# A quad's products reordered (rounded values first, low half last, two waits) and the weight preparation moved some steps later

## The reference

```
y      = layernorm(x), split in 16 heads of 8 columns
scores = y_h y_h^T / sqrt(8)             per batch and head, 1024 x 1024
o_h    = softmax(scores) @ y             y with all 128 columns
attn   = concat_h(o_h) @ weight          weight is (16*128, 128)
x      = x + layernorm(attn)
y      = layernorm(x); xr, xk = mixes of y and of y one row earlier
ffn    = sigmoid(xr W_r^T) * (relu(xk W_k^T)^2 W_v^T)
out    = x + layernorm(ffn)
```

## Time and profile before

| | us |
|---|---|
| median of 3 runs | 944.18 (943.57 to 948.45) |
| the profiled execution | 950.29 |
| span of its instructions | 948.5 |
| PE busy in the span | 914.9 (96%) |
| DVE busy | 850.3 (90%) |
| ACT busy | 753.4 (79%) |
| POOL busy | 320.2 (34%) |

### The profile page before, as it was taken

How to read it: one execution, slowest core, us unless ns; L and a number is a source line. 1 busy time by engine, 2 the same in 40 slices (tenths; PEclk the granted TensorE clock), 3 DMA queues, 4 the chain that set the end, 5 groups by cost and what they waited for, 6 DMA issues and landing times.

```text
span 948.5 us, 17874 instructions
## 1 busy us (share of the span) xinstructions
PE 914.9 (96%) x6065; PEld 441.9 (47%) x6065; DVE 850.3 (90%) x1117; ACT 753.4 (79%) x1048; POOL 320.2 (34%) x485
## 2 busy tenths in 40 slices
PE   3999999999999999999999999999999999999995
PEld 2444444444544444444444444544544444444453
DVE  7889898899898899989988979989889899898887
ACT  6787878788778778888778887889787978788855
POOL 2111432441143613515115282443313451153501
PEclk9999999999999999999999999999999999999999
DMA  5899999989889888999988978899988989889840
GB/s 162 195 225 188 205 197 200 226 190 204 177 173 201 163 181 174 208 193 207 185 178 179 203 157 179 176 222 202 206 173 180 188 182 188 172 179 201 174 81 24
DMA packets 98698, 173.12 MB, mean 183 GB/s; under 512 B 21040, under 2 KB 61360, under 8 KB 98608
## 3 DMA queue, kind: packets, MB, share of 16 engines
q0 software_dynamic: 36720, 133.71, 72.3%
q1 hardware_dynamic: 61888, 38.28, 14.7%
HBM read 27.72 MB, written 10.49 MB: 40 GB/s over the span
## 4 chain that ended last, share of the span: by engine, by line
PE 80%; issue 5%; POOL 4%; DVE 4%; DMA 4%; ACT 4%; DVEq 0%; POOLq 0%; ACTq 0%
PE ps_o L610 22%; PE ps_o L612 20%; PE ps_o L611 20%; PE ps_s L591 7%; DMA e_hi<-e_f 3%; PE ps_r L625 3%; PE ps_r L627 3%; PE ps_r L626 3%; ACT e_f L776 2%; DVE e_lo L1129 1%; POOL zT L452 1%; POOL e_hi L433 1%; PE ps_x L652 1%; PE ps_x L648 1%; POOL fnw L411 1%
## 5 line engine op out<-in xcount | busy, mean ns | idle before, releaser
L1129 DVE TENSOR_TENSOR e_lo<-e_f,e_hi 128x2048 f16<-128x2048 f32 x256 | 586.1, 2290 | 62.2 <-DMA e_hi<-e_f 62.1
L776 ACT ACTIVATE e_f<-ps_s 128x2048 f32<-128x2048 f32 x256 | 481.6, 1881 | 133.8 <-PE ps_s L591 124.4
L610 PE MATMUL ps_o<-e_hi,y_hi 128*128 128x512 f16 x1024 | 390.7, 382 | 6.3 <-DVE o_neg L1135 4.7
L612 PE MATMUL ps_o<-e_hi,y_lo 128*128 128x512 f16 x1024 | 388.1, 379 | 0.0
L611 PE MATMUL ps_o<-e_lo,y_hi 128*128 128x512 f16 x1024 | 388.1, 379 | 0.0
L433 POOL DMA_DIRECT2D e_hi<-e_f x255 | 140.9, 553 | 571.1 <-ACT e_f L776 469.8
L610 PEld LDWEIGHTS ps_o<-e_hi,y_hi 128*128 128x128 f16 x1024 | 99.7, 97 | 155.0 <-issue 56.1
L788 ACT ACTIVATE part<-ps_r,rden 128x128 f32<-128x128 f32 x508 | 144.8, 373 | 33.3 <-DVE rden L1141 32.6
L612 PEld LDWEIGHTS ps_o<-e_hi,y_lo 128*128 128x128 f16 x1024 | 100.2, 98 | 120.9
L611 PEld LDWEIGHTS ps_o<-e_lo,y_hi 128*128 128x128 f16 x1024 | 100.4, 98 | 91.5 <-issue 0.7
L591 PE MATMUL ps_s<-op_t,op_s 32*128 32x512 f16 x1024 | 102.5, 388 | 2.9 <-ACT e_f L776 2.4
(11 more groups left out here) (235 smaller groups left out, 507.4 us busy)
## 6 DMA issues: line engine op xcount, KB each, us to landing
e_hi<-e_f POOLq DMA_DIRECT2D x255, 512.0 KB, 5.1
op_t<-scr_t SPq DMA_DIRECT2D x496, 32.0 KB, 3.7
op_s<-scr_s SPq DMA_DIRECT2D x496, 16.0 KB, 3.3
scr_s<-yT SPq DMA_DIRECT2D x12, 256.0 KB, 2.9
scr_t<-yT SPq DMA_DIRECT2D x12, 256.0 KB, 5.4
out_dram<-res SPq DMA_DIRECT2D x7, 256.0 KB, 4.6
xs<-in_L_attn_x_dram SPq DMA_DIRECT2D x3, 512.0 KB, 6.2
scr_s<-eighth SPq DMA_DIRECT2D x4, 256.0 KB, 4.4
```

The lines of the kernel that those rows point to most:

```text
L610: nc.tensor.matmul(dst, y_hi[:, b % 2, s, :], e_hi[:, ring, g, :], start=(q == 0 and g == 0), stop=False)
L612: mm = nc.tensor.matmul(dst, y_lo[:, b % 2, s, :], e_hi[:, ring, g, :], start=False, stop=(q == 1 and g == 3))
L776: nc.scalar.activation(e_f[:, k % EF_RING], ps_s[:], ACT.Exp, scale=1.0 / ROOT).then_inc(weighed, 1)
L1129: dve.tensor_tensor(flat(e_lo[:, ring]), flat(e_f[:, k % EF_RING]), flat(e_hi[:, ring]), ALU.subtract).then_inc(split, 1)
```

## The change

Four things change, and the line numbers of the changed kernel are 4 to 11 higher than before.

1. **Products.** Of a quad's twelve matmuls the eight that read only `e_hi` come first, then the four that read `e_lo`. At the start PE now waits for the cast's DMA (`cast_in`, or `rounded` for quad 0), and a second wait, for `split`, stands ahead of the last four. `cast_count` is the count that DVE waited for before.
2. **Opening on PE.** `products(0)` moves from pass 4 to pass 3, ahead of the second `first_operands`; the four `weights_less` move behind it, the last one to pass 6; they use other banks, and `weight_sum` moves from pass 6 to pass 7.
3. **Weight preparation.** On DVE the four `weight_base` move to k = 3 to 6, `weight_scale` from k = 6 to 8, `weights_low` from 8 to 10. On ACT `keep_weight_sum` moves from 6 to 8, `weights_high` from 7 to 9, `weights_neg` from 8 to 10.
4. **`step_at`.** Step 0 now comes at lead+2, step 1 at lead+3, step 2 at lead+4: `project` at k = 10, 11, 12 (before 9, 10, 12), `invert` and `scale` at 11, 12, 13 (before 10, 11, 13).

```diff
         def weights_ps(i):
-            return (ps_o[:, 1, :], ps_o[:, 1, :], ps_r[:], ps_x[:])[i]
+            return (ps_o[:, 1, :], ps_r[:], ps_x[:], ps_r[:])[i]
 
         def step_at(k, lead):
 
-            if k == lead + 1:
-                return 0
-            return (k - lead) // 2 if k > lead and (k - lead) % 2 == 0 else None
+            if k in (lead + 2, lead + 3):
+                return k - lead - 2
+            return (k - lead) // 2 if k > lead + 3 and (k - lead) % 2 == 0 else None
...
+        def cast_count(k):
+
+            return 16 * (k // EH_RING + (k % EH_RING > 0))
...
                 if i == 1:
-                    pe.wait_ge(w_based, 1)
+                    pe.wait_ge(first_s_in, 2)
                 if i == 2:
-                    pe.wait_ge(first_s_in, 2)
+                    pe.wait_ge(first_t_in, 3)
                 if i == 3:
-                    pe.wait_ge(first_t_in, 3)
+                    pe.wait_ge(w_based, 2)
...
             def products(k):
                 j, q = k // 2, k % 2
                 b, ring = batch_of(j), k % EH_RING
-                pe.wait_ge(split, k + 1)
+                if k == 0:
+                    pe.wait_ge(rounded, 1)
+                else:
+                    pe.wait_ge(cast_in[ring], cast_count(k))
...
                 for g in range(4):
                     s = 2 * g + q
                     nc.tensor.matmul(dst, y_hi[:, b % 2, s, :], e_hi[:, ring, g, :], start=(q == 0 and g == 0), stop=False)
-                    nc.tensor.matmul(dst, y_hi[:, b % 2, s, :], e_lo[:, ring, g, :], start=False, stop=False)
-                    mm = nc.tensor.matmul(dst, y_lo[:, b % 2, s, :], e_hi[:, ring, g, :], start=False,
+                    nc.tensor.matmul(dst, y_lo[:, b % 2, s, :], e_hi[:, ring, g, :], start=False, stop=False)
+                pe.wait_ge(split, k + 1)
+                for g in range(4):
+                    mm = nc.tensor.matmul(dst, y_hi[:, b % 2, 2 * g + q, :], e_lo[:, ring, g, :], start=False,
                                           stop=(q == 1 and g == 3))
                 mm.then_inc(product, 1)
...
                 if k == LAG - 1:
+                    products(0)
+                    first_operands(1)
                     weights_less(0)
-                    first_operands(1)
+                if k == LAG:
                     weights_less(1)
-                if k == LAG:
                     weights_less(2)
-                    weights_less(3)
-                if 0 <= k - LAG < QUADS:
+                if 1 <= k - LAG < QUADS:
                     products(k - LAG)
                 if k == LAG + 2:
+                    weights_less(3)
+                if k == LAG + 3:
                     weight_sum()
...
-                if k == 6:
+                if k == 8:
                     keep_weight_sum()
-                if k == 7:
+                if k == 9:
                     weights_high()
-                if k == 8:
+                if k == 10:
                     weights_neg()
...
-                    weight_base(0)
-                    weight_base(1)
-                if k in (3, 4):
-                    weight_base(k - 1)
-                if k == 6:
+                if 3 <= k < 7:
+                    weight_base(k - 3)
+                if k == 8:
                     weight_scale()
-                if k == 8:
+                if k == 10:
                     weights_low()
```

More of the change, by code:

```diff
@@ L528, in weight_sum @@
                 pe.wait_ge(w_based, 3)
-                nc.tensor.matmul(ps_r[:, 0:1], ones[:], w_sum[:, 0:1], start=True, stop=True).then_inc(w_total, 1)
+                nc.tensor.matmul(ps_x[:, 0:1], ones[:], w_sum[:, 0:1], start=True, stop=True).then_inc(w_total, 1)
             def first_operands(n):
@@ L603, in products @@
                     if j == 1:
-                        pe.wait_ge(w_based, 2)
+                        pe.wait_ge(w_based, 1)
                     if j % (2 * H) == 0:
@@ L851, in keep_weight_sum @@
                 act.wait_ge(w_total, 1)
-                nc.scalar.activation(w_sum[:, 1:2], ps_r[:, 0:1], ACT.Copy).then_inc(w_summed, 1)
+                nc.scalar.activation(w_sum[:, 1:2], ps_x[:, 0:1], ACT.Copy).then_inc(w_summed, 1)
             def normalize_half():
@@ L1126, in split_quad @@
                 else:
-                    dve.wait_ge(cast_in[ring], 16 * (k // EH_RING + (ring > 0)))
+                    dve.wait_ge(cast_in[ring], cast_count(k))
                 ge(dve, product, k - EH_RING + 1)
```

## The result

| | us |
|---|---|
| changed kernel, median of 4 runs | 957.83 (955.8 to 958.6) |
| kernel before, median of 4 runs | 944.84 (943.57 to 948.45) |
| ratio, 95% interval | 1.0118 (1.0091 to 1.0145) |
| changed kernel, profiled execution | 957.83, span 956.0 |

A forecast was written before the change was run, and what follows sets the result against it. The prediction took PE, busy for 96% of the span, as the bound. Its terms, 0 (steady part) + 0.7 (opening) + 6.1 (first projection) = +6.8 us, on 944.2 gave 951.0 us, range 946.0 to 955.0.

The forecast's parts named there:

- The bound: Whole kernel: PE, busy for 96% of the span, sets the time; a 512-column matmul starts every 0.2155 us.
- Order and waits: Steady part: the new product order and its two waits cost 0, with 1.4 us of gain as the end.
- the wait for `e_lo` comes back at `o_neg`: Steady part: PE saves 1.38 us at `e_lo` but gives it back at `o_neg`, behind that `e_lo` in DVE's queue.
- The opening: Start to score group 8: early products run at the low clock; +0.7 us taken, between -1.0 and +1.5.
- The first projection: Score groups 8 to 13: `project(0)` waits 4.4 us for `w_lo`, later projections wait too; +6.1 us, from +4.6 to +8.6.
- the cast of quad 8: Ahead of `w_lo` in DVE's queue: the cast's DMA lands 5.8 us after issue, the median; fastest 4.3, slowest 8.3.
- The third projection: `project(2)` at k = 12 waits 2.5 us for `scale(1)`, which stands behind `f_turned` and `take_o(3)` on ACT.
- Against it: the gap is a little shorter than the one seen.: Ahead of `project(0)`: the 4.4 us gap is under the 4.6 us after which the clock fell at the end.
- Rival (a): Gap before `project(0)`: the clock falls to 1.2 GHz and PE loses 2.7 us more, 953.7 us; chance 0.20.
- The median of the runs lies 6.1 us below that execution; the difference carries over.: Whole kernel: +6.8 us gives 957.1 on the 950.3 us profiled execution, so 951.0 on the 944.2 us median.

The follow-up runs named there:

- order_only: The kernel before with only the new order of a quad's products and its two waits; ratio 1.0012 (0.9993 to 1.0031).
- twelve_waits: order_only with twelve more satisfied waits in each quad but the first, one ahead of each product; 946.75 us, ratio 0.9997 against the kernel before.
- opening_only: The changed kernel with the old order and old single wait of the products; ratio 1.0070 against the kernel before.
- low_k9: The changed kernel with `weights_low` one pass earlier on DVE (k = 9 instead of 10); 951.50 us, ratio 1.0048 against the kernel before.
- warm_gap: The changed kernel with 18 additional matmuls, results unused, ahead of the first projection; 951.29 us, ratio 1.0040 against the kernel before.
- old_times: The changed kernel with weight preparation and `step_at` passes as before, early products and new order kept; ratio 1.0013 against the kernel before.

## Why the prediction was right and wrong

**The bound, right.** PE's pace held at 0.2155 us for each product in every kernel, and everything lost was lost in waits of PE or at its lower clock.

**Order and waits: 0, right.** order_only and twelve_waits show it, and that the wait for `e_lo` comes back at `o_neg` was forecast and found in order_only (1.38 us gone at the first place, the wait at the second up from 1.06 to 2.24). In the changed kernel's own profile this sign did not appear: its longest wait for `o_neg` is 0.9 us.

**The opening: +0.7, about right, in part by luck.** Profiles with the early products have score group 8 between 40.9 and 42.2 us, those without between 40.8 and 41.8. In the changed kernel the first eight products stood 0.40 to 0.43 us apart, so they did run at the low clock, and so did the last four (25.05 to 26.73). The sum had eight slow and four fast; for twelve slow ones the prediction had +1.5:

```profile
21.66 0.61 PE L617 MATMUL ps_o<-e_hi,y_hi 128*128 128x512 f16 x1
22.06 0.64 PE L618 MATMUL ps_o<-e_hi,y_lo 128*128 128x512 f16 x1
...
27.53 1.12 PE L574 MATMUL ps_o<-w_raw,less 128*128 128x512 f32 x2
28.83 0.40 PE L595 MATMUL ps_s<-op_t,op_s 32*128 32x512 f16 x4 [0.18 <-issue]
```

The transposes behind them took 0.8 us (26.73 to 27.53) instead of the 1.4 of the sum, and the weight product at 27.53 took 1.30 us to the next group, against 2.0 before: what the products lost there, the later work of PE got back.

**The first projection: +6.1, the mechanism right, the size 1 to 2 us short.** `project(0)` was forecast 13.3 us after score group 8 and came 14.4, 12.8 and 14.6 us after it in the three profiles; its wait was forecast at 4.4 us and was 5.25, 3.70 and 5.41. The term that was mis-sized is the cast of quad 8. The sum took 5.8 us for it and a wait 1.4 us shorter. It took 6.9, 5.4 and 7.1 us in these profiles (5.6 in opening_only, with a wait of 3.91), and the wait was 1.7 us shorter than it each time. Group 8 to 13 was forecast at 25.2 us and took 27.3, 26.3 and 27.0. The third projection waited 2.25 us for 2.5.

**The step that failed first: "Against it: the gap is a little shorter than the one seen."** Rival (a) got 0.20 on that ground, and the sum was made without it. Its sign, products 0.43 us apart behind the gap, is what came. The clock fell in the gap in all four profiles that had one of 3.7 us or more (three of the changed kernel, one of opening_only), 2.1 to 2.7 us after PE went idle, not 4.6. One row at the end of the program was read as a delay that must pass. It showed one case. The price of (a), 2.7 us, was too high instead: 0.8 to 1.8 us were lost behind the gap.

**The step that failed second: "The median of the runs lies 6.1 us below that execution; the difference carries over."** The difference of +6.8 us did hold in the two later comparisons (7.2 and 6.7, whole kernels). But the level of 944.2, from three runs, and the range around it did not. The next 65 executions of the kernel before had medians from 946.9 to 949.9, and one that was profiled took 954.4. The single profile at 950.29 looked odd beside three numbers and was nothing special. A range of 946 to 955 around a sum should have held this spread of the kernel, and did not. Against 957.83 the sum was 6.8 us low, and 6.1 us of it are this step: on the profiled execution the same sum gave 957.1, and the changed kernel's profiled execution, which is also its median, took 957.83. That those two lie so close is in part luck. Between the two profiles there are 0.2 us up to group 8 (forecast 0.7), 8.1 from 8 to 13 (forecast 6.1), 2.1 given back from 13 to 255 and 1.3 more in the ending (neither forecast). Why the four executions of the kernel before lay so far under its later levels stays open.

**What gives a little back** is likely but not shown: from group 13 to 255 the seven profiles with late placement took 839.9 to 846.2 us, the five others 842.8 to 850.1. The two overlap, so it may be chance. In low_k9 and warm_gap this stretch also holds 0.9 and 1.4 us of the second fall of the clock.

## What to carry to other kernels

When a step is moved later on an in-order engine, write down what it now stands behind. Here `w_lo` passed a low half that waits for a DMA, and all but 1.7 us of the DMA's time became a wait of the engine that bounds the kernel. A wait removed from the bounding engine is worth only what its next wait doesn't take back, and the next wait is found by following the engine that was late. Before a forecast of under 1%, ask how far the same kernel's executions lie apart: three runs said 5 us, 65 more showed a median 2.7 to 5.7 us higher. And where a clock can fall, look past the place of the experiment: two of the runs moved the fall instead of removing it.

## What the runs showed of the hardware

A satisfied wait ahead of a matmul cost PE nothing measurable, with one ahead of each of the twelve products of 255 quads (946.75 us beside 946.89). The extra 0.09 us was seen where the operand's shape changes from 128 rows to 32.

Once it had risen after the opening, the granted clock fell in every wait of 3.7 us and more, and in or just behind some shorter ones. In low_k9 PE was idle from 61.2 ahead of the third projection, and the clock was down at about 63.3. In warm_gap, behind the same wait of 2.25 us, it fell half a microsecond after PE had begun again; in the changed kernel itself it stayed up there. In old_times it fell at 562.7, one microsecond after PE had resumed behind waits of 0.59 and 1.55 us. In the ending it fell in eight profiles of twelve, with no wait of PE over 1.2 us near it. So a gap's length alone does not tell whether the clock falls, and the same kernel can do either. In the Trainium skill, "TensorE: Matmul & The Clock Gate", the example under "Seeing it yourself" has the fall 5.2 us after the last matmul. Here it came 2.1 to 2.7 us after PE went idle in the long gaps, so the delay of one profile can't be used as a safe margin in another.
